# A fused attention and feed-forward kernel: the order of score and selector matmuls in the turned scores

## The reference, cut to what matters

```
qh, kh, vh = proj(q), proj(ctx), proj(ctx)      # (b, 16, s, 8, 4), then x + 0.1*amp*x@interference
scores = einsum('bhqdm,bhkdm->bhqkm', qh, kh) / sqrt(8)
weights = softmax(scores, axis=3)
out = einsum('bhqkm,bhkdm->bhqdm', weights, vh)
x = x + out @ Wo.T + bo
x = x + ffn(layernorm(x))                        # silu(gate) * up, weights unpacked from 4 bits
```

## Time and profile before

| what | before |
|---|---|
| median of 3 executions | 880.54 us |
| the profiled execution's own time | 883.46 us |
| its span | 881.7 us |
| TensorE busy | 798.8 us, 91% |
| VectorE / ScalarE / GpSimd busy | 487.5 / 427.4 / 296.9 us |
| mean granted clock of TensorE | 0.938 |

### The profile page before, as it was taken

How to read it: one execution, slowest core, us unless ns; L and a number is a source line. 1 busy time by engine, 2 the same in 40 slices (tenths; PEclk the granted TensorE clock), 3 DMA queues, 4 the chain that set the end, 5 groups by cost and what they waited for, 6 DMA issues and landing times.

```text
span 881.7 us, 24230 instructions
## 1 busy us (share of the span) xinstructions
PE 798.8 (91%) x10119; PEld 569.5 (65%) x10119; DVE 487.5 (55%) x1000; ACT 427.4 (48%) x817; POOL 296.9 (34%) x297
## 2 busy tenths in 40 slices
PE   5465778899999999999999999999999999999898
PEld 5411324565787578757875787578757876787484
DVE  9878563453656465646564656465646564644421
ACT  1656566353665166516651665166516652565020
POOL 2155355243144304430443044304430443054020
PEclk9755666999999999999999999999999999999899
DMA  8943122000100110011001100110011000100000
GB/s 281 261 107 93 52 72 84 26 3 1 52 2 4 50 52 2 3 50 52 2 3 50 52 3 3 50 51 3 3 50 49 5 3 25 28 2 15 13 1 25
DMA packets 21509, 37.09 MB, mean 42 GB/s; under 512 B 4158, under 2 KB 8414, under 8 KB 21404
## 3 DMA queue, kind: packets, MB, share of 16 engines
q1 hardware_dynamic: 21404, 35.48, 13.7%
HBM read 26.47 MB, written 4.19 MB: 35 GB/s over the span
## 4 chain that ended last, share of the span: by engine, by line
PE 69%; DVE 10%; issue 8%; ACT 7%; SPq 2%; DMA 1%; POOL 1%; DVEq 0%; ACTq 0%; POOLq 0%
PE bank L556 17%; PE bank L571 13%; PE bank L527 10%; PE bank L537 9%; PE bank L696 4%; PE bank L713 3%; DVE nmf L1274 3%; PE bank L583 3%; PE bank L690 3%; ACT arena L917 3%; PE bank L504 2%; PE bank L671 2%; DVE arena L1206 1%; DVE stats L1211 1%; SPq L377 1%
## 5 line engine op out<-in xcount | busy, mean ns | idle before, releaser
L556 PE MATMUL bank<-arena,WGU 128*128 128x256 f16 (+1 forms) x2112 | 248.2, 274 | 1.4 <-DVE arena L761 1.4
L556 PEld LDWEIGHTS bank<-arena,WGU 128*128 128x128 f16 (+1 forms) x2112 | 206.9, 101 | 27.9 <-DVE arena L761 1.6
L1462 POOL TENSOR_TENSOR arena<-arena 128x512 f16<-128x512 f32 x128 | 146.8, 1173 | 209.5 <-ACT arena L924 209.5
L571 PE MATMUL bank<-WD,arena 128*128 128x512 f16 (+1 forms) x528 | 121.0, 379 | 0.0
L917 ACT ACTIVATE arena<-bank,small 128x512 f32<-128x512 f32 x128 | 89.1, 775 | 58.6 <-PE bank L696 58.6
L1452 POOL TENSOR_TENSOR arena<-arena 128x512 f16<-128x512 f32 (+1 forms) x48 | 51.6, 1076 | 181.3 <-ACT arena L900 181.3
L527 PE MATMUL bank<-arena,WT 128*128 128x256 f16 x768 | 90.5, 280 | 11.6 <-issue 9.1
L527 PEld LDWEIGHTS bank<-arena,WT 128*128 128x128 f16 x768 | 76.8, 100 | 25.4 <-issue 14.3
L537 PE MATMUL bank<-WT,arena 128*128 128x512 f16 x384 | 87.2, 384 | 0.0
L571 PEld LDWEIGHTS bank<-WD,arena 128*128 128x128 f16 (+1 forms) x528 | 49.4, 97 | 53.2
L1274 DVE TENSOR_REDUCE nmf<-bank 128x8 f32<-128x512 f32 x128 | 79.3, 681 | 5.5 <-PE bank L671 5.3
(11 more groups left out here) (172 smaller groups left out, 1049.2 us busy)
## 6 DMA issues: line engine op xcount, KB each, us to landing
arena<-in_L_ffn_qweight_gu SPq DMA_DIRECT2D x8, 688.0 KB, 5.4
arena<-arena SPq DMA_DIRECT2D x32, 144.0 KB, 2.6
WT<-in_ctx SPq DMA_DIRECT2D x8, 512.0 KB, 10.0
arena<-in_ctx SPq DMA_DIRECT2D x8, 512.0 KB, 4.0
arena<-in_x SPq DMA_DIRECT2D x8, 512.0 KB, 3.5
out_y<-arena SPq DMA_DIRECT2D x16, 256.0 KB, 2.1
arena<-in_L_ffn_qweight_down SPq DMA_DIRECT2D x10, 256.0 KB, 3.5
arena<-in_L_xattn_Wk SPq DMA_DIRECT2D x1, 1024.0 KB, 5.5
```

The source lines that it names most:

```text
L556: mm = e.matmul(pb[0:m, i * TOK:(i + 1) * TOK], WGU[:, sp, kb, half * INTER + fb * P:half * INTER + fb * P + m], x2T[:, mp, kb, :], start= ...
L571: mm = e.matmul(pb[:, :], hT[0:m, sp, fb, t * P:(t + 1) * P], WD[0:m, mp, fb, :], start=(n == 0), stop=(n == 3 * FB - 1))
L1462: e.tensor_tensor(phl[:, a, 1, :], pring[:, a, :], phl[:, a, 0, :], ALU.subtract).then_inc(S["p_lo"], 1)
```

## The change

In `pe_scores_turned` the four selector matmuls of a block i no longer follow the twelve score matmuls of that block. All 48 score matmuls of the batch are issued first (i = 0..3), then all 16 selector matmuls (i = 0..3). There is one accumulation group per bank now: only the very first matmul of each bank has `start=True` (before, the first of each block did), and only the last of each bank has `stop=True`. The same 64 matmuls are issued with the same operands, the wait on `nm_ready` stands ahead of them as before, and the semaphore increments are still on the last four selector matmuls.

```
--- before.py
+++ after.py
@@ -690,10 +690,11 @@
                         e.matmul(AB[a][:, i * P:(i + 1) * P],
                                  km[rows, kp, NB * i + b, :, :].rearrange("p v t -> p (v t)"),
                                  qm[rows, qp, NB * i + b, :, :].rearrange("p v t -> p (v t)"),
-                                 start=(n == 0), stop=False)
+                                 start=(i == 0 and n == 0), stop=False)
+            for i in range(KB):
                 for a in range(4):
                     rows = slice(32 * a, 32 * a + 32)
-                    mm = e.matmul(AB[a][:, i * P:(i + 1) * P], sel[rows, i, :], nmT[rows, :], start=False, stop=True)
+                    mm = e.matmul(AB[a][:, i * P:(i + 1) * P], sel[rows, i, :], nmT[rows, :], start=False, stop=(i == KB - 1))
                     if i == KB - 1:
                         mm.then_inc(S["st_done"], 1)
```

## The result

The changed kernel takes 870.55 us (median of 6 executions, 869.24 to 872.79) against 880.25 us for the kernel before (median of 6, 878.45 to 883.99): a ratio of 0.989, 95% interval 0.9864 to 0.9915. The profiled execution took 869.85 us, its span 868.1; against the profiled one of before the gain is 13.6 us. So two amounts have to be explained: 5.1 us forecast, and 4.6 (medians) or 8.5 (profiled executions) more.

The account below looks back on a forecast made before the run. TensorE, busy 91% of the span, was taken to bound the kernel. Saving 3 x 0.053 = 0.16 us a batch, times 32, gave 5.1 us: 880.54 - 5.1 = 875.4 us, 0.58% faster; range 874.0 to 880.7.

Parts of the forecast that it names:

- the direct term: Turned scores on TensorE: three of four fp16-to-fp32 changes go, 0.16 us saved a batch, 5.1 us over 32 batches.
- the forecast mechanism: Selector matmuls: first fp32 pass behind an fp16 group costs 0.165 us, behind an fp32 group 0.112; chance 0.80.
- the unchanged waits for the maxima: TensorE's waits for the next batch's maxima after turned scores: forecast to stay at 11.4 us in 13 waits.
- the fold: Plain fp32 matmuls back to back on 128 rows, stepping at 0.111 us; taken as nearest row for the grouped selector matmuls.
- (b): Rival: fp32 selector groups on 32 rows step at 0.138 us, so time stays at 880.5 us; chance 0.07.
- (c): Rival: the 0.053 us stall comes at every fp32 selector group, 1.27 us against 1.11, 885.6 us; chance 0.05.
- (a): Rival: later TensorE waits (maxima, perhaps loop heads) eat the gain, 877.5 us, at most 880.5; chance 0.08.
- The rule that I set beside (c): Skill rule: weight loads overlap matmuls in flight only where the row group differs; by it (c) would be the forecast.
- the waits at the loop's head: TensorE's five waits at the loop's head, 9.1 us in all, taken as a fixed delay; at most 3.2 us lost otherwise.
- the half-clock stretch at the end: Granted clock 0.50 from 831.3 to 837.9 us, costing 2.7 us; inferred to explain the profiled execution's 2.9 us above median.

## Why the prediction was wrong, point by point

**Right: the direct term, and with it the forecast mechanism.** Every piece of it was found: 1.73 us for a batch, the median of 270 ns, one record in eight long, the unchanged waits for the maxima, no effect of the flags, 12 fp16 groups at the old step. 32 x 0.16 = 5.1 us stand in the profile, the rounds without a wait differ by 0.63 us for four batches, and the medians with 16 idle instructions by 5.7 us. The choice of the fold as the row for fp32 behind fp32 held on 32 rows too, so rivals (b) and (c) fall; (a) falls as the gain of the batches reached the round. What each change from fp16 to fp32 costs is measured (0.053 us). The reason given for it, a load of 186 ns without cover, is argued: the run with the selectors first counts against its simple form. The rule that I set beside (c), "TensorE: Matmul & The Clock Gate", Part 3, What overlaps and what doesn't of the Trainium skill, does not agree with this trace: fp32 groups of four on the same rows follow each other at 0.112 us, which the 0.95 us of eight passes show, and a load of 186 ns could not stand between two of them.

**Wrong: the waits at the loop's head.** The step that failed says of them "I take them as a fixed delay behind the last instruction of the chunk before". They were 9.1 us in the very view that I quoted, with no releaser that the profile names, and I weighed only that they might eat the gain (rival (a)), never that they could go. They fell to 1.2 us. The term is missing from the sum, with the sign of a gain: -7.9 us against the profiled execution, about -4.6 against the median. The second is less than the first, as I read it, because the kernel before loses the race in some rounds only: 4.6 / 1.7 is about three rounds of five. That count is worked out from medians. It fits the spread: at granted clocks of 0.937 and 0.938 the kernel before took 874.0 to 880.6 us, while the old order with 16 idle instructions and no waits took 874.8 and 875.3 at 0.937; in steps of 1.7 us that is none to about three waits. The five profiled executions with the old fourth batch and no more than 4 idle instructions have 5, 3, 5, 5 and 4 waits, and four of the five lie above the median of their kernel.

**Wrong: what part of the change matters for them.** "No instruction is added or removed, no wait, no DMA" was true of the program and not of the execution: five instruction packets went, and with them the waits. A step that only moves instructions moved the moment at which the sequencer asks for code.

**Wrong: how the profiled execution stood to the median.** I put its 2.9 us down to the half-clock stretch at the end and called it an inference. The profiled execution of after, one of its three fastest, has the same stretch:

```profile
817.10:823.70 6.60, 5.19 (x25) 3.54 (x25) 1.38 (x2) 0.66 (x2) 0.00 (x0) 0.50 0.01 2
```

So that stretch is in short executions too, and does not explain the 2.9 us. Nor was the clock of the profiled execution of before low: 0.938, where its other executions have 0.932 to 0.940. Five lost races against about three (two more, 3.4 us) would: its five waits stand in its profile, and 875 us, the old order without waits, and 5 x 1.7 us are 883.5 us, where it took 883.46. The number in the others is worked out, not shown.

**Open.** The 14 profiled executions have 70 jumps back to a loop's head. In 22 of them the extra packet starts within 0.3 us of the one with the head, and there TensorE waits 1.7 to 2.0 us. In the other 48 it comes 1.8 us or more ahead, or not at all, and no wait is over 0.41 us. The 22 are among the 25 jumps with the old order in the fourth batch and at most 4 idle instructions; none is among the 25 with the new order there. So it is shown that this order decides whether the two packets can go out together, that the wait goes with the pair, and that a shift of 16 instructions cures the old order.

Not shown is how the order of 64 matmuls, some 15 us ahead of the branch, comes to move the request. The number of the last instruction alone does not decide: the new order had no extra packet at 5117 and at 5121, the old one had it at both. Nor is it shown how a packet holds TensorE up: the later of the two packets lands about 1.1 us later than a single one, and TensorE's wait is 1.6 us longer. About 1.3 us that both orders lose with 64 idle instructions are open as well.

## What to carry to other kernels

Where a matmul's weight load takes longer than the matmul ahead of it, try to group the matmuls with the slow loads: here the price of a change from fp16 to fp32, 0.053 us, was then paid once a batch and not four times, in 32 batches. Count and measure the changes; what stands ahead of the group matters too (0.053 us behind fp16 groups on 32 rows, 0.10 behind 128-row matmuls). A wait marked "issue" at a loop's head is not a constant: look at the queue that carries instructions, count its packets per round, and where two start together at the branch try a shift of a few instructions first; here 16 idle ones gave the old order 3.7 us, and 64 only 1. And before a gain of 1% is put down to a reordering inside a hardware loop, run the reordering at another shift or the old order at several.

## What the runs showed of the hardware that was not expected

TensorE's code is read during the execution, 16384 bytes at a time. One packet alone took about 1 us, two together 1.8 us each on average, and with the two at the branch TensorE idled 1.7 us longer in that round. Which of the two happens can change from round to round within one execution. With 64 idle instructions a further wait of 0.18 to 0.59 us came 29 matmuls behind the head. A first fp32 pass on 32 rows behind 128-row fp16 matmuls took 372 ns, behind an fp16 group on 32 rows 323, behind another fp32 group 270.
